# Flamingo block on one core: row sums of ctx sent by way of memory, first two samples in another order

## The reference, cut to what matters

```python
x = x + tanh(g_xattn) * xattn(layernorm(x), ctx, ctx, Wt, Wp, Wg, Wz, gn_w, gn_b)
x = x + tanh(g_ffn) * ffn(layernorm(x), A_w, B_w, Wq_w, keys)

# xattn, for each of 8 samples, C = 256 channels, D = 1024, 8 groups of 32 channels
t, p, g = Wt @ v, Wp @ q, Wg @ k               # q = layernorm(x), k = v = ctx
att = sum over a group of (p * g)               # one number per group
y = blockdiag(Wz) @ (att * t)
xattn = groupnorm(y) * gn_w + gn_b + ctx
# ffn: router scores from 16 numbers per row, top 16 of 64 experts, softmax gate
out = ((x @ A_w.T) * gate repeated 8 times) @ B_w.T * 2
```

## Time and profile before

| | us |
|---|---|
| median of 3 runs | 373.27 (373.02 to 373.32) |
| profiled execution, its time | 372.22 |
| its span in the profile | 370.4 |
| PE busy | 334.5 (90%) |
| DVE busy | 281.9 (76%) |
| ACT busy | 155.2 (42%) |
| POOL busy | 151.6 (41%) |
| a steady iteration (z_product(0,b) to the next) | 39.97 |

### The profile page before, as it was taken

How to read it: one execution, slowest core, us unless ns; L and a number is a source line. 1 busy time by engine, 2 the same in 40 slices (tenths; PEclk the granted TensorE clock), 3 DMA queues, 4 the chain that set the end, 5 groups by cost and what they waited for, 6 DMA issues and landing times.

```text
span 370.4 us, 5694 instructions
## 1 busy us (share of the span) xinstructions
PE 334.5 (90%) x2104; PEld 306.9 (83%) x2104; DVE 281.9 (76%) x672; ACT 155.2 (42%) x253; POOL 151.6 (41%) x100
## 2 busy tenths in 40 slices
PE   5963279639999999999999999999999999999996
PEld 4862279628899889998999889988998899988984
DVE  2596586966968987798969896898689895787352
ACT  4535186325544265317613554435541761136110
POOL 0053266722656344661586065635466248000000
PEclk9995569959999999999999999999999999999999
DMA  7960475333641536061813364153706140001102
GB/s 258 348 238 0 170 264 192 112 114 113 186 158 33 195 110 230 2 212 53 252 56 89 139 199 144 54 174 113 228 1 226 58 174 0 2 1 58 57 28 87
DMA packets 14924, 47.50 MB, mean 128 GB/s; under 512 B 1824, under 2 KB 1952, under 8 KB 14896
## 3 DMA queue, kind: packets, MB, share of 16 engines
q1 hardware_dynamic: 14544, 46.93, 37.2%
q10 hardware_dynamic: 352, 0.20, 0.2%
HBM read 38.74 MB, written 8.39 MB: 127 GB/s over the span
## 4 chain that ended last, share of the span: by engine, by line
PE 81%; DVE 10%; DMA 4%; ACT 2%; issue 2%; SPq 1%; DVEq 0%; ACTq 0%
PE z_ps L860 24%; PE w_ps L887 24%; PE w_ps L809 11%; PE w_ps L778 9%; PE t_ps L848 4%; PE z_ps L821 3%; DMA uw<-in_cT 3%; DVE B_lo L522 2%; PE t_ps L874 2%; PE w_ps L860 2%; DMA raw<-in_xT 1%; PE t_ps L791 1%; DVE u_st L570 1%; DVE x_st L536 1%; DVE c_sb L529 1%
## 5 line engine op out<-in xcount | busy, mean ns | idle before, releaser
L278 POOL TENSOR_TENSOR xT_lo<-raw,xT_hi 128x1024 fp32r<-128x1024 f32 x14 | 41.8, 3003 | 32.1 <-ACT xT_hi L360 32.1
L887 PE MATMUL w_ps<-B_hi,zT_hi 128*128 128x512 f32 x128 | 52.7, 411 | 0.0
L887 PE MATMUL w_ps<-B_hi,zT_lo 128*128 128x512 f32 x128 | 50.3, 393 | 0.0
L887 PE MATMUL w_ps<-B_lo,zT_hi 128*128 128x512 f32 x128 | 50.0, 391 | 0.0
L860 PE MATMUL z_ps<-A_hi,hT_hi 128*128 128x288 f32 x224 | 49.0, 301 | 0.0
L860 PE MATMUL z_ps<-A_lo,hT_hi 128*128 128x288 f32 x224 | 48.3, 297 | 0.0
L860 PE MATMUL z_ps<-A_hi,hT_lo 128*128 128x288 f32 x224 | 48.2, 297 | 0.0
L860 PEld LDWEIGHTS z_ps<-A_hi,hT_hi 128*128 128x128 f32 x224 | 36.8, 191 | 0.5
L860 PEld LDWEIGHTS z_ps<-A_hi,hT_lo 128*128 128x128 f32 x224 | 36.4, 190 | 0.0
L860 PEld LDWEIGHTS z_ps<-A_lo,hT_hi 128*128 128x128 f32 x224 | 36.4, 190 | 0.0
L397 ACT ACTIVATE uw<-w_ps,neg_u 128x512 f32<-128x512 f32 x32 | 20.3, 685 | 37.8 <-DVE neg_u L575 37.8
(11 more groups left out here) (147 smaller groups left out, 820.9 us busy)
## 6 DMA issues: line engine op xcount, KB each, us to landing
...
raw<-in_aT SPq DMA_DIRECT2D x4, 256.0 KB, 2.8
raw<-in_bT SPq DMA_DIRECT2D x4, 256.0 KB, 5.8
```

The lines of the kernel that those rows point to most:

```text
L278: pool.tensor_tensor(xT_lo[:, half_of(h), :], raw[:, half_of(h), :], xT_hi[:, half_of(h), :].bitcast(f32), ALU.subtract).then_inc(xT_lo_s, 1)
L887: last = pe.matmul(w_ps[k][:, :], z[:, t, row], w[:, j, cols], start=(j == 0 and z is zT_hi and w is B_hi), stop=(j == KN - 1 and z is zT_lo))
```

## The change

1. `ctx_sums` and `cb_copy` are gone. `spread_sums` on SP writes the column `c_sum` to memory, waits for that, and reads it back broadcast to all partitions into `cb_sb`. `gram_fix` waits for the second transfer (`cb_in`). In sample 0 it stands ahead of the loads of the A lots, in sample 1 between lots 13 and 14, later at the head of an iteration. The next `c_high` waits for the first one (`sums_out`).
2. gram(1) goes to the banks `z_ps`, and u_product(1) no longer waits for M_low(1).
3. `scale_ctx` on ACT now computes tanh(g)·ctx + beta for samples 0 and 1, and `x_add` on POOL adds x. POOL's two passes of sample 0, and x_shift and x_plus_ctx of sample 1, are gone.
4. The lists of samples 0 and 1 are reordered on ACT, DVE, POOL and SP: the scalar constants and the router's `A_lo` on DVE come later, `gram_fix(0)` and `M_low(0)` ahead of the lots, hT_high(0,0) ahead of xT_high(.,1), lots 3 to 7 behind hT_low(0,0), x of sample 1 is loaded ahead of xT, lots 8 and 9 come from `stage`, and lots 12 to 15 are split after M_high(1) and M_low(1). The loads of xT for sample 2 now wait for 14 lots instead of 12. POOL takes y_root(1) between the two xT_low of sample 2.

The diff, cut to its core:

```diff
         def gram_bank(n, t):
-            return z_ps[t] if n == 0 else w_ps[t]
+            return z_ps[t] if n < 2 else w_ps[t]
...
-                        sp.wait_ge(lot_lo_s, KN if n == 1 else KD + KN)
+                        sp.wait_ge(lot_lo_s, KN if n == 1 else KD + 2 + KN)
...
+            def spread_sums(n):
+
+                sp.wait_ge(c_hi_s, per_tile(n, T - 1))
+                sp.dma_start(sums[n].rearrange("t p -> p t"), c_sum[:, :], allow_slow_non_contiguous=True).then_inc(sums_out, 16)
+                sp.wait_ge(sums_out, 16 * (n + 1))
+                if n > 0:
+                    sp.wait_ge(M_fixed, per_tile(n - 1, T - 1))
+                sp.dma_start(cb_sb[:, :].rearrange("p (t q) -> p t q", t=T),
+                             sums[n].unsqueeze(0).to_broadcast([P, T, P])).then_inc(cb_in, 16)
...
+            spread_sums(0)
             for j in range(KD - 2):
                 load_lot(j)
...
+            load_x(1)
             load_xT(1)
-            load_x(1)
             load_c(1)
             load_cT(1, 1)
+            for j in range(KD, N_LOTS - 2):
+                load_lot(j)
+            spread_sums(1)
             for j in range(N_LOTS - 2, N_LOTS):
-                load_lot(j)
-            for j in range(KD, N_LOTS - 2):
                 load_lot(j)
             load_xT(2)
             for b in range(NB - 1):
+                if b > 0:
+                    spread_sums(b + 1)
...
+            def x_add(n):
+                for t in range(T):
+                    pool.wait_ge(c_scaled, per_tile(n, t))
                     pool.tensor_tensor(c_sb[:, t, :], c_sb[:, t, :], x_sb[:, t, :], ALU.add).then_inc(xt_done, 1)
...
+                    act.wait_ge(sums_out, 16 * n)
                 act.wait_ge(c_in[t], 16 * (n + 1))
...
+            def scale_ctx(n):
+                act.wait_ge(beta_done, n + 1)
+                act.wait_ge(c_lo_s, per_tile(n, T - 1))
+                for t in range(T):
+                    act.activation(c_sb[:, t, :], c_sb[:, t, :], ACT.Identity, scale=tg[:, 0:1],
+                                   bias=beta[:, t:t + 1]).then_inc(c_scaled, 1)
...
-                dve.wait_ge(cb_s, n + 1)
+                dve.wait_ge(cb_in, 16 * (n + 1))
...
+            gram_fix(0)
+            M_low(0)
+            lot_low(0)
+            lot_low(1)
+            dve.wait_ge(wg_in, 16)
+            att_reduce(0)
+            group_deviation(0)
+            slopes(0, lambda: lot_low(2))
+            w_tiles(0)
+            offsets(0)
             dve.wait_ge(router_hi_s, 1)
             dve.tensor_tensor(A_lo[:, :, NN:ZC], t_ps[0][:, :].rearrange("p (k e) -> p k e", k=KD),
                               A_hi[:, :, NN:ZC].bitcast(f32), ALU.subtract).then_inc(router_lo_s, 1)
...
             hT_low(0, 0)
-            for j in range(KN, KD):
+            for j in range(3, KD):
                 lot_low(j)
...
                 if b == 0:
-                    for j in range(KD, KD + KN):
-                        lot_low(j)
+                    lot_low(KD)
+                    lot_low(KD + 1)
                     gate(1, b, w_ps[NH:USES])
                     zT_low(0, b)
-                    for j in range(KD + KN, N_LOTS):
-                        lot_low(j)
-                    x_plus_ctx(m)
+                    lot_low(KD + 2)
+                    lot_low(KD + 3)
                 gram_fix(m)
                 M_low(m)
-                if b > 0:
+                if b == 0:
+                    for j in range(KD + 4, N_LOTS):
+                        lot_low(j)
+                else:
                     zT_low(0, b)
...
             def u_product(n):
-                if n > 0:
+                if n >= 2:
                     pe.wait_ge(M_lo_s, per_tile(n, T - 1))
```

More of the change, by code:

```diff
@@ L323, in _ @@
             x_root(0)
-            x_plus_ctx_first()
+            x_add(0)
             y_root(0)
@@ L451, in _ @@
                            ACT.Copy).then_inc(router_hi_s, 1)
[L452 to L454 removed]
+            lot_high(0)
+            lot_high(1)
+            scale_ctx(0)
             u_copy(0)
[L456 removed]
+            M_high(0)
+            for j in range(2, KD):
                 lot_high(j)
[L458 to L460 removed]
+            hT_high(0, 0)
             for h in range(NH):
                 xT_high(h, 1)
[L463 removed]
             hT_high(1, 0)
@@ L767, in _, with gram @@
         def _(pe):
-            def gram(n, between):
+            def gram(n):
                 for t in range(T):
@@ L910, in _ @@
             u_product(0)
-            ctx_sums(0)
-            gram(0, lambda: None)
+            gram(0)
             group_means(0)
```

124 lines of the change are left out of this document (47 added, 77 removed).

## The result

| | before | changed |
|---|---|---|
| median of 4 runs, us | 373.14 (372.73 to 373.32) | 389.43 (386.27 to 389.53) |
| ratio, 95% interval | | 1.0409 (1.0385 to 1.0433) |
| profiled execution, its time / span | 372.22 / 370.4 | 389.48 / 387.7 |
| z_product(0,1) starts | 102.1 | 111.2 |
| z_product(0,b) to the next, b = 1 to 5 | 39.97 (all five) | 42.06, 41.60, 41.02, 41.39, 42.13 |

The forecast was 368.9, with a range of 363.5 to 371.8. Where the 17.3 us between the two profiled executions arose can be read from the starts of z_product(0,b): 9.1 by b = 1, another 8.4 from b = 1 to b = 6 (319.44 - 111.24 against 301.94 - 102.10), and -0.2 from there to b = 7; behind it the two programs take the same time. So both halves of the forecast failed: the head lost 9.1 where 1.8 was to be won, and the steady part lost 8.2 where 2.6 was.

What follows compares the result with a forecast made beforehand. PE was taken to bound steady iterations, and waits for other engines and loads the head. Savings of 1.8 us in the head and 2.6 steady, 4.4 in all, took 373.27 to 368.9 us, range 363.5 to 371.8.

Steps and rivals of the forecast that it cites:

- the head: Samples 0 and 1, up to z_product(0,1): filling PE's holes there was to save 1.8 us.
- the steady part: Samples 2 to 7: ctx_sums leaves PE, 6 x 0.44 = 2.6 us saved, with the round trip through memory costing nothing.
- (a): Sums of sample 0: first write lands at 18.0 us (bounds 17.3 and 24.6), lot 0 at 21.3.
- (b): M(0): ACT's lots, scalings and copies, then M_high and M_low, put n_product(0) at 28.4 us, 5.4 earlier.
- (c): hT(0,0) at 39.6 us, 3.4 earlier, as PE waits for the router's A_lo behind w_tiles and offsets on DVE.
- (d): hT_high(0,0) no longer behind xT_high: z_product(0,0) at 43.6 us, 6.6 earlier.
- (h): Lots 12 and 13 release xT of sample 2, u_copy(1) stands behind xT_high: out_product(0,0) at 82.0 us, 7.2 earlier.
- (j): POOL's y_root(1) ahead of the second xT_low delays hT(1,1): z_product(0,1) at 100.5 us, 1.8 earlier.
- Rival 3: Round trip late for gram_fix every iteration, excess above 9.8 us paid about in full six times; at 12 us, 382; chance 0.06.
- (e): Gain given back: xT of sample 1 loads late, beta(1) at 55.4 us, zT(0,0) waits until 59.4, 5.2 earlier.
- rival 4: M(1)'s four DVE lots beside POOL each wait a whole pass, 3.3 us instead of 1.7: 375.1 us; chance 0.02.
- (i): PE starts cold at out_product(0,0), behind the wait for u_copy(1): 1.6 us paid again.

Runs made afterwards that it cites:

- Experiments 4: The changed kernel with the column written as 128 pieces of 8 bytes and read as one row of 1 KB: 375.39 us, ratio 1.0059.
- 5: Kernel before, with single transfers in a quiet queue behind its last work: 256 4-byte pieces took 8.5 us side by side, 1.6 set 512 bytes apart.
- 7: The changed kernel with each column written as 128 pieces of 16 bytes and read as rows of 2 KB: 374.20 us, ratio 1.0005.
- experiment 3: The changed kernel with the column written from ACT's DMA queue instead of SP's: 394.32 us, ratio 1.0519.
- experiments 1: The changed kernel's order alone, with the sums put back on PE and ACT (ctx_sums, cb_copy): 370.46 us, ratio 0.9919 to the kernel before.
- 2: The kernel before with the sums by way of memory and nothing else changed: 384.16 us, ratio 1.0287.
- 6: Changed order, sums through memory only in sample 0: 381.26 us; only in samples 2 to 7: 384.14; the latter in 8-byte pieces: 368.83.
- (i): Changed order, 8-byte pieces in samples 2 to 7, sums on PE in 0 and 1, plus router's A_lo ahead of gram_fix(0): 367.32 us, ratio 0.9843.
- (iii): (i) plus, in iteration 0, u_copy(1) ahead of xT_high, w_square(1) between the cT_high, and both xT_low of sample 2 ahead of y_root(1): 363.17 us.

## Why the prediction was wrong

Positions in us; the order alone has its sums on PE.

| step | forecast | changed | with 16-byte pieces | order alone |
|---|---|---|---|---|
| (a) first write landed | 18.0 | 22.6 | 17.5 | |
| (a) lot 0 landed | 21.3 | 28.0 | 23.2 | |
| (b) n_product(0) | 28.4 | 35.3 | 30.5 | 26.4 |
| (c) hT(0,0) | 39.6 | 46.1 | 41.4 | 35.8 |
| (d) z_product(0,0) | 43.6 | 50.3 | 45.6 | 40.0 |
| (h) out_product(0,0) | 82.0 | 91.7 | 87.2 | 81.5 |
| (j) z_product(0,1) | 100.5 | 111.2 | 106.9 | 101.3 |
| steady iteration | 39.5 | 41.6 | 39.5 | 39.97 |

**The step that failed: the price of the trip.** "I take about 7 ... so the store's row is the nearer." It was 12.9 in the mean. The bounds held (4.9 to 15.9), but the value in them came from a 256 KB store because the queue would be quiet, and no row of before had pieces of 4 bytes. The other row, 7.5 us for a load in 128 small pieces, wasn't nearer: its pieces have 24 bytes, and 16-byte pieces took 1.4 to 2.3 us alone and 8.8 behind the first loads, so its 7.5 may well have been its company, as the prediction had it. That twice this row gave a bound that held is luck. Experiments 4, 5 and 7 show the form as the cause of the steady price, experiment 3 and the quiet queue that company is not.

Rival 3 is what happened in the steady part, with its place. Its rule that the excess is paid "about in full" was right as well; only the point of decision was 10.7 and not 9.8, and 13.5 in the last iteration. So the first five trips (mean 12.8) cost 2.1 each (8.4 plus the 2.2 saved on PE), and the last (13.7) cost 0.2. With 12.9 us in its sum rival 3 would give 388, close to what was measured, but by two errors that nearly cancel: 8 us too much in the steady part, 11 too little in the head. The range left out a cost that its own bounds allowed: a chance of 0.06 for it was far too small when the value lay 2.8 us from the point of decision and the bound 6.1 beyond it.

The Trainium skill's page "DMA: Bandwidth & Descriptors", section Rules for kernel authors, was right in kind, that a strided last dimension means one descriptor per element. But a count of descriptors doesn't give these prices: 256 of them took 1.6 us with gaps and 8.5 without. Nor do the 2 us of fixed time in the Trainium skill's page "DMA: Bandwidth & Descriptors", section Anatomy of one DMA, which gives them for transfers issued by GpSimd, while these are issued by SP.

**(a), first write.** 18.0 was right for the place in the queue: 17.5 with 16-byte pieces. The rest to 22.6 is the 4-byte form again. Lot 0 was given 2.8 to land and took 5.0 in the changed kernel and 5.3 with 16-byte pieces; why isn't shown. Together 4.6 + 2.2 = 6.8, which is the 6.9 that n_product(0) was late. The effect is amplified by the order: experiments 1, 2 and 6 (the first trip alone: z_product(0,1) 9.7 later) put the head's loss by the first trip at 10 in the new order and nothing up to n_product(0) in the old, where both early trips together cost 1.2 by z_product(0,1).

**(b), (c).** From lot 0 to n_product(0) 7.1 were forecast and 7.3 measured, from there to hT(0,0) 11.2 and 10.8. The wait for the router's A_lo was real, and (i) shows its price.

**(e) to (h).** 42.4 us from hT(0,0) to out_product(0,0) were forecast, 45.6 measured. Two terms of DVE beside POOL were too small, the two lots beside c_low and the gate. From the changed kernel's DVE timeline:

```profile
65.64 2.00 DVE L679 TENSOR_TENSOR g_scale<-g_rec,w_rs 128x1 f32<-128x1 f32 x1
68.47 2.70 DVE L541 TENSOR_TENSOR B_lo<-stage,B_hi 128x512 fp32r<-128x512 f32 x1
71.08 2.86 DVE L541 TENSOR_TENSOR B_lo<-stage,B_hi 128x512 fp32r<-128x512 f32 x1
77.46 0.68 DVE L541 TENSOR_TENSOR B_lo<-raw,B_hi 128x512 fp32r<-128x512 f32 x1
78.06 2.89 DVE L541 TENSOR_TENSOR B_lo<-raw,B_hi 128x512 fp32r<-128x512 f32 x1
```

The two lots beside POOL's c_low take 5.48 us together, where 3.4 were forecast. They start at 68.47 and 71.08, while c_low's two passes run (68.23 to 70.61 and 70.56 to 73.40), and each ends 0.5 to 0.6 behind its pass. Of the two beside x_add, the first starts ahead of the pass (at 77.71) and takes 0.68, the second starts within it and takes 2.89. And g_scale, on 128 x 1 elements, takes 2.00 beside POOL's cT_low, where the other 15 gates have it at 0.16 to 0.79. Lots and g_scale together are 3.8 more, and the measured gap is 3.2.

So the mechanism of rival 4 was at work at three of its four places, and the earlier trace rows had not spoken against it. "6.89 for four" was read as 1.72 each, but it is a sum of two kinds. One by one, in the kernel before:

```profile
62.56 0.69 DVE L522 TENSOR_TENSOR B_lo<-raw,B_hi 128x512 fp32r<-128x512 f32 x1 [1.62 <-ACT B_hi L437]
63.17 2.88 DVE L522 TENSOR_TENSOR B_lo<-raw,B_hi 128x512 fp32r<-128x512 f32 x1
65.98 2.87 DVE L522 TENSOR_TENSOR B_lo<-raw,B_hi 128x512 fp32r<-128x512 f32 x1
68.77 0.68 DVE L522 TENSOR_TENSOR B_lo<-raw,B_hi 128x512 fp32r<-128x512 f32 x1
```

Two lots there waited for a pass of c_low and two for none. "SBUF — State Buffer" in the Trainium skill, section Who interferes with whom, has the rule, two SBUF inputs on DVE against a reading POOL instruction, and one waits for the whole of the other; the trace agrees at these five lots and g_scale.

Two positions of the forecast don't follow from the parts given with them: beta(1) at 55.4, where the parts give 54.1, and the end of u_product(1) at 71.6, where 66.8 + 5.46 is 72.3. Neither is what failed: from hT(0,0) to beta(1) 15.8 were forecast and 15.8 measured.

**(i), (j).** From out_product(0,0) on, 18.5 were forecast and 19.5 measured. y_root(1) did stand in front (its xT_low ran at 96.5), but (iii) shows nothing to be had there once u_copy is early.

**What held.** Steady iterations of 39.53 when the trip fits, and no M_lo wait ahead of u_product(1). The order alone reached z_product(0,1) at 101.3 against 100.5, though its parts were off against each other: n_product(0) 2 us earlier, the middle 3 longer.
